# Last attention product of an eight-core transformer block: softmax sums and output normalization kept in PSUM

## The reference, cut to what matters

```
def sandwich(x):
    y = attention(layernorm(x))            # q, k, v = linear; softmax(q k^T / 8 + mask) v; linear Wp
    x = x + layernorm(y)
    f = layernorm(x) @ W[idx] + b[idx]     # idx: argmax of log_softmax(logits) + gumbel(u)
    return x + layernorm(f)
# mask: causal, and every fourth key column (3, 7, 11, ...) left out
```

## Time and profile before

| | |
|---|---|
| time before, median of 3 runs | 746.71 us (746.45 to 749.49) |
| the profiled execution's own time | 743.47 us |
| its span, core 6 (slowest) | 741.9 us |
| spans of the 8 cores | 740.7, 733.8, 737.9, 734.6, 741.3, 735.9, 741.9, 739.7 us |
| busy share of the span | PE 88%, ACT 72%, DVE 56%, POOL 19% |
| chain that ended last, by engine | PE 50%, ACT 15%, issue 15%, DMA 11%, DVE 6% |

### The profile page before, as it was taken

One profiled execution on the slowest core, in us unless ns is written; L12 is line 12 of the kernel. 1 busy time (PEld: TensorE's weight loads), 2 busy tenths in 40 slices (PEclk: granted clock), 3 DMA queues, 4 the chain that ended last, 5 costly groups with the idle time before them and its releaser, 6 DMA issues.

```text
span 741.3 us, 24579 instructions; the slowest of 8 cores (733.8 to 741.9 us)
## 1 busy us (share of the span) xinstructions
PE 649.0 (88%) x9452; PEld 283.8 (38%) x9460; DVE 418.1 (56%) x744; ACT 530.2 (72%) x718; POOL 144.0 (19%) x238
## 2 busy tenths in 40 slices
PE   1788989889898999999999998889999999999846
PEld 1444435344344444333433433333333333333312
DVE  3327766765655463653333333277766776986484
ACT  3233356344698787888878888888898989888246
POOL 1010013122122112212111124110120110760104
PEclk9979999899999999999999999999999999999989
DMA  8989467955357062123400035602233223142224
GB/s 161 185 184 159 147 173 154 208 83 109 99 115 165 18 132 44 32 46 55 93 17 17 18 59 84 190 16 74 83 77 88 75 88 105 34 138 87 102 57 142
DMA packets 78240, 72.47 MB, mean 98 GB/s; under 512 B 58544, under 2 KB 58800, under 8 KB 78128
## 3 DMA queue, kind: packets, MB, share of 16 engines
q1 hardware_dynamic: 72060, 59.50, 31.9%
q0 software_dynamic: 5696, 11.14, 9.6%
q10 hardware_dynamic: 372, 0.27, 0.2%
HBM read 60.68 MB, written 8.52 MB: 93 GB/s over the span
## 4 chain that ended last, share of the span: by engine, by line
PE 50%; ACT 15%; issue 15%; DMA 11%; DVE 6%; SPq 1%; ACTq 1%; POOL 1%; DVEq 0%; POOLq 0%
PE pj L673 23%; ACT Pr L1223 12%; PE sps L744 10%; PE yz L781 7%; PE yz L799 4%; DMA wkb<-wk 3%; DMA wvb<-wv 2%; PE yz L671 2%; DMA fmQ<-tok 1%; PE pj L671 1%; PE sps L847 1%; DVE Vsb L901 1%; DMA zr<-zev 1%; DMA xq<-xkv 1%; DMA xq<-xq 1%
## 5 line engine op out<-in xcount | busy, mean ns | idle before, releaser
L1223 ACT ACTIVATE Pr<-sps,negc 128x1024 bf16<-128x1024 f32 (+1 forms) x416 | 428.8, 1078 | 92.7 <-PE sps L746 90.1
L1354 POOL TENSOR_TENSOR Pr<-Pr,mk_sb 128x172 bf16<-128x172 bf16 x192 | 98.9, 536 | 464.8 <-ACT Pr L1223 464.7
L744 PE MATMUL sps<-QY,Ksb 64*128 64x512 bf16 (+2 forms) x480 | 138.7, 346 | 25.2 <-ACT Pr L1223 23.2
L746 PE MATMUL sps<-QY,Ksb 64*128 64x512 bf16 (+2 forms) x480 | 140.4, 350 | 0.0
L781 PE MATMUL yz<-Pr,Vsb 128*32 128x512 bf16 (+5 forms) x1920 | 125.0, 345 | 5.8 <-POOL Pr L1354 3.2
L744 PEld LDWEIGHTS sps<-QY,Ksb 64*128 64x128 bf16 x480 | 35.8, 93 | 133.5 <-issue 131.2
L799 PE MATMUL yz<-Pr,cbf 128*32 128x512 bf16 (+2 forms) x960 | 82.0, 345 | 0.0
L781 PEld LDWEIGHTS yz<-Pr,Vsb 128*32 128x32 bf16 x1920 | 49.4, 97 | 49.3 <-issue 12.5
L901 DVE TENSOR_TENSOR Vsb<-pj,bvb 128x512 bf16<-128x512 f32 x41 | 28.1, 688 | 52.4 <-PE pj L673 46.7
L673 PE MATMUL pj<-wpb,QY 128*32 128x512 bf16 x768 | 50.7, 381 | 0.1
L673 PE MATMUL pj<-fmQ,wqb 128*32 128x512 bf16 x768 | 48.0, 388 | 2.2 <-DMA fmQ<-tok 2.2
(11 more groups left out here) (195 smaller groups left out, 807.8 us busy)
## 6 DMA issues: line engine op xcount, KB each, us to landing
xin<-xkv SPq DMA_DIRECT2D x21, 512.0 KB, 4.7
xr<-xq SPq DMA_DIRECT2D x16, 512.0 KB, 3.4
zb<-zscr SPq DMA_DIRECT2D x62, 128.0 KB, 3.3
xin<-xq SPq DMA_DIRECT2D x12, 512.0 KB, 4.4
out<-xr SPq DMA_DIRECT2D x12, 512.0 KB, 2.8
wkb<-wk POOLq DMA_DIRECT2D x4, 512.0 KB, 17.8
wvb<-wv POOLq DMA_DIRECT2D x2, 1024.0 KB, 15.8
wqb<-wq POOLq DMA_DIRECT2D x2, 1024.0 KB, 14.2
```

What stands on the lines that cost most here:

```text
L744: PE.matmul(sps[s % 2][:, 0, off:off + w], Ksb[0:64, g, hp, kc:kc + 128], QY[0:64, t, hp, n0:n0 + w], start=True, stop=True, tile_position ...
L746: mm = PE.matmul(sps[s % 2][:, 1, off:off + w], Ksb[64:128, g, hp, kc:kc + 128], QY[64:128, t, hp, n0:n0 + w], start=True, stop=True, tile ...
L1223: A.activation(out=Pr[:, s % 4, :, 0:wide], in_=sps[s % 2][:, :, 0:wide], func=AF.Exp, bias=negc[:, k:k + 1], scale=0.125).then_inc(s_exp, 1)
L1354: op = G.tensor_tensor(out=view, in0=view, in1=mk[:, j:j + 1, :].broadcast_to([128, 2, BAND]), op=ALU.mult)
```

## The change

In product 31 the sums are laid out as the values are: for each step and each of the four groups of 32 partitions a matmul with the block of ones (`last_rowsum`), so that `zps` holds at each place the sum that belongs to the value at that place of `yps`. VectorE then takes the reciprocal from PSUM and multiplies, for 128 query columns at a time (`last_norm`); the copies and transfers of product 31 are gone. `tail_o` ends both halves of a subtile right after it has begun them. The masks of the last pass, 207, go from GpSimd to VectorE (`last_mask`). The end of every queue is no longer given by planned times but listed entry by entry (`behind`). The offsets of products 0 to 30 are written out rounded.

```diff
--- before.py
+++ after.py
@@ -256,11 +256,12 @@
             dve.append((x + 0.2, "fadd", u[1:]))
             if u[2] == 1:
                 f_free = x + 1.2 + 6.1
-                dve.append((x + 1.2, "fstat", u[1]))
-                act.append((x + 1.2 + 4.0, "froot", u[1]))
-                dve.append((x + 1.2 + 6.0, "final", u[1]))
-                sp.append((x + 1.2 + 9.0, "store", u[1]))
-                if u[1] + 4 < 16:
+                if u[1] < 11:
+                    dve.append((x + 1.2, "fstat", u[1]))
+                    act.append((x + 1.2 + 4.0, "froot", u[1]))
+                    dve.append((x + 1.2 + 6.0, "final", u[1]))
+                if u[1] < 10:
+                    sp.append((x + 1.2 + 9.0, "store", u[1]))
                     sp.append((x + 1.2 + 12.0, "resid", u[1] + 4))
     for s in range(4):
         sp.append((start[3] - 1.0 + 0.01 * s, "resid", s))
@@ -293,36 +294,34 @@
         for a in range(2):
             x = begin[m] + 0.4 + 1.1 * a
             act.append((x, "exp", 2 * m + a))
-            if masked(2 * m + a):
+            if masked(2 * m + a) and m < NP - 1:
                 pool.append((x + 1.1, "mask", 2 * m + a))
-    for k in range(32):
-        x = begin[LAST[k] + 2] if LAST[k] + 2 <= NP else begin[NP] + 1.0
+    for k in range(31):
+        x = begin[LAST[k] + 2]
         dve.append((x, "ycopy", k))
-        by, late = (sp, 1.35) if k < 31 else (act, 1.0)
-        by.append((x + 1.4, "zrow", k))
-        dve.append((x + 4.2 * late, "zinv", k))
-        by.append((x + 4.6 * late, "zout", k))
-        by.append((x + 7.6 * late, "zback", k))
+        sp.append((x + 1.4, "zrow", k))
+        dve.append((x + 5.7, "zinv", k))
+        sp.append((x + 6.2, "zout", k))
+        sp.append((x + 10.3, "zback", k))
         again = begin[LAST[k + 2] + 2] - 0.3 if k < 29 else begin[NP] + 20.0
-        dve.append((min(x + 13.5 * late, again), "ynorm", k))
-
-    at = begin[NP] + 16.0
-    z_at, x_at, f_at, last_at = [0.0, 1.4, 5.2, 9.0], [2.8, 6.6, 10.4, 12.8], [15.2, 16.6, 18.0, 22.0], [17.2, 18.6, 20.2, 24.0]
-    for j, s in enumerate(TAIL):
-        dve.append((at + z_at[j], "tailz", s))
-        act.append((at + z_at[j] + 1.4, "tailzroot", s))
-        dve.append((at + x_at[j], "tailx", s))
-        act.append((at + x_at[j] + 2.4, "tailln", s))
-        sp.append((at + x_at[j] + 4.5, "turn", s))
-        dve.append((at + f_at[j], "tailfs", s))
-        act.append((at + f_at[j] + 1.4, "tailfroot", s))
-        if s < 15:
-            act.append((at + last_at[j], "tailscale", s))
-            pool.append((at + last_at[j] + 0.6, "tailsum", s))
-        else:
-            dve.append((at + last_at[j], "taillast", s))
-            act.append((at + last_at[j] + 0.6, "tailout", s))
-        sp.append((at + last_at[j] + 1.2, "tailstore", s))
+        dve.append((min(x + 18.2, again), "ynorm", k))
+
+
+    late = max(begin[NP], max(item[0] for item in dve)) + 1.0
+
+    def behind(queue, *items):
+        queue.extend((late + 0.01 * n, kind, key) for n, (kind, key) in enumerate(items))
+
+    behind(dve, ("lastmask", 0), ("lastmask", 1), ("fstat", 11), ("lastnorm", 12), ("lastnorm", 13), ("lastnorm", 14),
+           ("tailz", 12), ("lastnorm", 15), ("tailx", 12), ("tailz", 13), ("final", 11), ("tailx", 13), ("tailz", 14),
+           ("tailz", 15), ("tailx", 14), ("tailx", 15), ("tailfs", 12), ("tailfs", 13), ("tailfs", 14), ("tailfs", 15),
+           ("taillast", 15))
+    behind(act, ("froot", 11), ("tailzroot", 12), ("tailln", 12), ("tailzroot", 13), ("tailln", 13), ("tailzroot", 14),
+           ("tailzroot", 15), ("tailln", 14), ("tailln", 15), ("tailfroot", 12), ("tailscale", 12), ("tailfroot", 13),
+           ("tailscale", 13), ("tailfroot", 14), ("tailscale", 14), ("tailfroot", 15), ("tailout", 15))
+    behind(pool, ("tailsum", 12), ("tailsum", 13), ("tailsum", 14))
+    behind(sp, ("store", 10), ("resid", 14), ("turn", 12), ("store", 11), ("resid", 15), ("turn", 13), ("turn", 14),
+           ("turn", 15), ("tailstore", 12), ("tailstore", 13), ("tailstore", 14), ("tailstore", 15))
     for i in range(3):
         pool.append((begin[FIRST[30]] + 1.0 + 9.0 * i, "biasrow", i))
     pool.append((-400.0, "weights", 0))
@@ -565,6 +564,8 @@
     s_zout = sem("s_zout")
     s_zback = [sem(f"s_zback{i}") for i in range(2)]
     s_ynorm = sem("s_ynorm")
+    s_lastmask = sem("s_lastmask")
+    s_lastinv = sem("s_lastinv")
     s_res = [sem(f"s_res{i}") for i in range(4)]
     s_zadd = sem("s_zadd")
     s_zbn = sem("s_zbn")
@@ -766,7 +767,9 @@
                 if k > 0:
                     PE.wait_ge(s_ycopy, k)
             for s in (2 * m, 2 * m + 1):
-                if masked(s):
+                if s >= 2 * NP - 2:
+                    PE.wait_ge(s_lastmask, s - 2 * NP + 3)
+                elif masked(s):
                     PE.wait_ge(s_mask, MASK_N[s])
                 else:
                     PE.wait_ge(s_exp, s + 1)
@@ -781,12 +784,27 @@
                             PE.matmul(yps[j:j + 32, n0:n0 + w], Vsb[:, c, 64 * h + 32 * half:64 * h + 32 * half + 32],
                                       Pr[:, s % 4, hd, off:off + w], start=first, stop=final, tile_position=(0, j))
 
+        def last_rowsum(m):
+
+            for s in (2 * m, 2 * m + 1):
+                for c, n0, w, off in STEPS[s][1]:
+                    first = s == 2 * FIRST[31]
+                    final = s == 2 * LAST[31] + 1 and off + w == 428
+                    for j in (0, 32, 64, 96):
+                        mm = PE.matmul(zps[j:j + 32, n0:n0 + w], cbf[:, 288:320], Pr[:, s % 4, j // 64, off:off + w],
+                                       start=first, stop=final, tile_position=(0, j))
+            return mm
+
         def rowsum(m):
 
             k, _ = STEPS[2 * m]
             first, final = m == FIRST[k], m == LAST[k]
             if first and k > 0:
                 PE.wait_ge(s_zcopy, k)
+            if k == 31:
+                mm = last_rowsum(m)
+                mm.then_inc(s_pv, 1)
+                return
             if first and k < 8:
                 for hd in range(2):
                     PE.matmul(zps[64 + 32 * hd:96 + 32 * hd, :], cbf[:, 320:352], Pr[:, 2 * m % 4, hd, :],
@@ -824,19 +842,12 @@
             if s == 14:
                 PE.wait_ge(s_exp, 2 * NP)
             if s == 15:
-                PE.wait_ge(s_ycopy, 32)
-                PE.wait_ge(s_zcopy, 32)
+                PE.wait_ge(s_ynorm, 35)
             tail_begin(s, 0)
-            if s < 15:
-                tail_begin(s, 1)
-            else:
-                PE.wait_ge(s_ynorm, 32)
-                for r in (12, 13, 14):
-                    tail_end(r, 0)
-                    tail_end(r, 1)
-                tail_end(15, 0)
-                tail_begin(15, 1)
-                tail_end(15, 1)
+            tail_begin(s, 1)
+            PE.wait_ge(s_ynorm, s + 20)
+            tail_end(s, 0)
+            tail_end(s, 1)
 
         def tail_f(s):
             PE.wait_ge(s_tturn[s - 12], 16)
@@ -990,6 +1001,25 @@
             t, hp = k // 8, k % 8
             V.wait_ge(s_zback[k % 2], 32 * (k // 2 + 1))
             V.tensor_tensor(out=QY[:, t, hp, :], in0=yev[:, k % 2, :], in1=zb[:, k % 2, :],
+                            op=ALU.mult).then_inc(s_ynorm, 1)
+
+        def last_mask(a):
+            s = 2 * NP - 2 + a
+            V.wait_ge(s_mk, 16)
+            V.wait_ge(s_exp, s + 1)
+            for c, _, _, off in STEPS[s][1]:
+                view = Pr[:, s % 4, :, off:off + BAND]
+                op = V.tensor_tensor(out=view, in0=view, in1=mk[:, c - 18:c - 17, :].broadcast_to([128, 2, BAND]),
+                                     op=ALU.mult)
+            op.then_inc(s_lastmask, 1)
+
+        def last_norm(s):
+
+            n0, n1 = 128 * (s - 12), 128 * (s - 11)
+            V.wait_ge(s_pv, NP)
+            V.reciprocal(out=zev[:, 1, n0:n1], in_=zps[:, n0:n1]).then_inc(s_lastinv, 1)
+            V.wait_ge(s_lastinv, s - 11)
+            V.tensor_tensor(out=QY[:, 3, 7, n0:n1], in0=yps[:, n0:n1], in1=zev[:, 1, n0:n1],
                             op=ALU.mult).then_inc(s_ynorm, 1)
 
         def zadd(key):
@@ -1143,6 +1173,10 @@
                 fstat(key)
             elif kind == "final":
                 final(key)
+            elif kind == "lastmask":
+                last_mask(key)
+            elif kind == "lastnorm":
+                last_norm(key)
             elif kind == "tailz":
                 tail_z(key)
             elif kind == "tailx":
@@ -1307,22 +1341,6 @@
                 x1root(key)
             elif kind == "froot":
                 froot(key)
-            elif kind == "zrow":
-                A.wait_ge(s_zcopy, key + 1)
-                for a in range(2):
-                    A.dma_start(out=zr[:, key % 2, a, :], in_=zev[64 * a:64 * a + 64:32, key % 2, :]
-                                ).then_inc(s_zrow[key % 2], 16)
-            elif kind == "zout":
-                A.wait_ge(s_zinv, key + 1)
```

(9 more changed lines are left out.)

## The result

The changed kernel takes 741.78 us (median of 5 runs, 740.27 to 742.84) against 746.71 us (745.7 to 749.49), a ratio of 0.9927 with a 95% interval of 0.9902 to 0.9952: 0.7% faster, 742.5 was forecast. The profiled execution took 742.84 us.

A forecast was written before the change was run, and what follows sets the result against it. TensorE mostly sets the pace before the tail; in it product 31's DRAM trip, then VectorE's queue, bound the kernel. Terms +0.9 before the tail, −6.1 in it, +1.0 clock: −4.2 us, median 742.5, range 738.0 to 747.2.

The forecast's parts named there:

- What bounds what: In the tail, after the change, VectorE's queue from the norms to tailx 15 is what is late.
- the trip's 12.7 us: Product 31's copies and DRAM transfers: removing them isn't 12.7 us gained, since 56 of 64 opening matmuls ran meanwhile.
- Sums: Product 31's passes before the tail: doubled sum matmuls cost +1.4 us, bounds +0.7 to +2.3.
- P: Start of the tail's first matmul, 691.29 us before the change; forecast to move by +0.9 us.
- Masks: Last pass: masks on VectorE take about 0.3 us each and bring P −0.5 us, bounds −0.8 and 0.
- Norms: Tail on VectorE: reciprocal 1.1 us, wait 0.1, multiply 0.3, so 1.5 us for each of four subtiles.
- Clock: TensorE's clock in the tail: three new pauses may slow F 14, up to 2.5 us; allowed +1.0.
- Sum: Whole kernel: +0.9 before P, −6.1 after it, +1.0 for the clock, −4.2 us, median 742.5.
- Queue order: Rounded offsets swap zback 6 and feature 28 on SP; costs nothing, 1.3 us at most without cover.
- A: Rival in the tail: reciprocal takes only 0.36 us, later steps gain 2.5, −6.7 us, 740.0; chance 0.17.
- B: Rival in the tail: TensorE stays at 1.2 GHz through F, slower than before, 751.7; chance 0.06.
- C: Rival in the tail: reciprocal takes 2 us and sums the full +2.3, leaving about 0, 746.5; chance 0.15.

The follow-up runs named there:

- experiment 5: Changed kernel with each of the four reciprocals issued twice; P to the end 46.9 to 47.6 us on four cores, 48.5 to 49.0 on four.
- experiment 8: Changed kernel with tailz 14 earlier and final 11 moved from VectorE to ScalarE and GpSimd; 736.25 us, ratio 0.9914 to the kernel before.
- experiment 2: Changed kernel with output halves in the old order (12, 13, 14 all begun, then ended, then 15); ratio 1.0012 to the kernel before.
- experiment 3: Changed kernel with only half the sum matmuls in product 31's nine full passes; that stretch 24.01 to 24.02 us, P to the end 43.57 to 44.03.
- experiment 1: Changed kernel with the last pass's masks back on GpSimd; q-k products to the end 47.77 us, against 47.76 with masks on VectorE.
- experiment 6: Changed kernel with eleven useless matmuls in each TensorE pause before F 13 and F 14; P to the end 44.12 us.
- experiment 4: Changed kernel with copies of the same size instead of the four reciprocals; P to the end 43.13 us, −0.94.
- experiment 10: The changed kernel run again, unaltered, beside the best version; 740.16 us, ratio 0.9931 to the kernel before.
- experiment 7: Changed kernel, reordered only: tailz 14 ahead of final 11 and tailx 13, its root ahead of tailln 13; ratio 0.9933 to the kernel before.
- experiment 9: Final 11 off VectorE with tailz 14 earlier, plus eight useless matmuls in TensorE's pause before F 13; 736.19 us, ratio 0.9887 to the kernel before.

## Why the prediction was right, step by step

- *What bounds what.* VectorE's queue from the norms to tailx 15 is late, as forecast: experiments 5 (+3.2 at F 13 for longer norms) and 8 (−1.9 for 2.2 us less) move the end from that queue; experiment 2 shows the other half of the statement, that the trip's 12.7 us were no gain while TensorE's opening matmuls stood ahead of the first end.
- *Sums.* Forecast +1.4 in all, between +0.7 and +2.3; measured +1.09 up to the last q-k products, which experiment 3 takes away exactly, and 0.19 from there to P (4.31 in experiment 1 against 4.12), 1.28 in all. The first part holds the nine full passes, priced at 9 × 0.22: 0.9 of these 1.98 us were swallowed. Of that the rows show 0.4 as idle time that went (TensorE is idle 1.66 of 24.02 us before and 1.30 of 25.10 after); where the rest went, they don't show, as ends of matmuls are modelled. The second part holds the sums of passes 206 and 207, priced at 0.18 and 0.15; those of 206 end before TensorE waits for the last masks, and cost nothing.
- *Masks.* Forecast −0.5 in P, with 0.3 given back behind it: fstat 11 ends at P + 0.9, "the sums are there at 0.6, as now". The operation was sized right (0.24 each against 0.3) and P came sooner by 0.62, but the step that failed is this 0.6. Before the change it was the start of the copy of the values; the reciprocal could start 0.16 us after P (experiment 1), and behind fstat it started at 0.77. So 0.61 us are given back of 0.62, and the masks' term is 0 for the end instead of −0.2.
- *Norms.* Forecast 1.1 + 0.1 + 0.3, measured 0.94 + 0.1 + 0.29, and the next instruction starts slightly before the end: 1.26 from one norm to the next instead of 1.5. That is nearly all of the difference in the chain: tailz 12 at 4.53 (5.45), F 12 at 16.3 (17.4), F 13 at 22.8 (24.05), F 14 at 29.1 (30.4), the end at 43.6 on core 4 (44.5 without the clock). The median end is 44.07, as on five cores F 15's turn comes 0.1 to 0.5 us after F 14 is done, a wait that the prediction did not have. The reciprocal grows with its length: 16 values (from SBUF, 64 partitions) 0.244 us, 128 values (from PSUM, 128 partitions) 0.94, 6.2 ns more for each. Of the two rules of the Trainium skill that the prediction set against each other ("VectorE: DVE Perf Modes"), the formula of its errata section, an estimate of 0.26 us, fits the copy (0.27) and not the reciprocal; the divide repeated 8 times, an estimate of 1.07 us and more, is the nearer one, though the measured 0.94 lies below it.
- *Clock.* Forecast +1.0, measured about 0 for the end. F 13 was the slow one and covered: F 14 starts at the same time after P with it slow or quick, and experiment 6, with both quick, ends no sooner. That a slow F 14 costs 1.5 us and more was right and shows in experiments 4 and 5. Not forecast: before, P to the end is 1.3 to 2.1 us longer on the three cores with a slow clock after P; after, all are within 0.75 us.
- *Sum.* P moved by +1.28 − 0.62 = +0.66 (+0.9 forecast), the tail by −5.2 (−6.1 + 1.0 forecast). That the sum comes within 1 us is in part luck. The end was forecast 45.5 us after P and came at 44.07, 1.4 too late, from the norms' price and the clock; but it was taken from the 50.6 of core 6, one of the three with the slow clock after P, where the median core had 49.27, 1.3 less. The two errors cancel. On core 6 itself the tail became 6.8 us shorter, not 5.1.
- *Queue order.* No run separates the rounded offsets of products 0 to 30. Product 30's last values start at 660.6 us before (median of the cores), 662.4 after and 660.5 in experiment 10, single cores anywhere from 656 to 669: no cost stands out of that spread, and none is excluded below it.
- *Rivals.* A (cheap reciprocal) would have been worth 0.94 us against the measured kernel, or 1.4 against the forecast 44.5, not the 2.5 that it was given (experiment 4): TensorE's output and the root of tailz 12 take over at once. B (a slow clock through F) did not come. C (a reciprocal of 2 us) is nearly what experiment 5 imitates: P to the end is 46.9 to 49.0 there against 49.27 before, and P comes 0.66 us later, which would have left little.

## What to carry to other kernels

Taking a round trip off a path frees only what was not being used meanwhile: what ran under the wait (here 56 matmuls) must be cut into pieces whose first result starts the next stage, or the gain is gone (experiment 2). An operation moved from an idle engine to the one that is late is priced by that engine's queue, not by the wait that it shortens. When a queue is the bound, look for work in it that idle engines can do, even in more steps: 2.2 us moved from VectorE to ScalarE and GpSimd (4.6 us there) gave 1.9. And a forecast that starts from the slowest core should first ask whether that core's stretch is the others' too: here 1.3 us of its tail were not.

## What the runs showed of the hardware

- A reciprocal of 128 float32 values from PSUM takes 0.93 to 0.95 us, a copy of the same tile 0.27, the multiply 0.29.
- A 2 × 86 mask in bfloat16 takes 0.24 us on VectorE, 0.46 to 0.55 on GpSimd.
- After a pause of 2.5 us TensorE's next F half took 2.7 to 3.6 us on six cores and 1.94 on two of the same execution (the changed kernel, F 13); after one of 4.0 us 3.4 to 3.8 on all eight (experiment 7); with eight matmuls without use in the pause 1.94 on all eight (experiment 9). Why before the change three cores had a clock of 0.5 after P and in experiment 1, with the same masks on GpSimd, none had, stays open: each is one execution. The rows show one difference, that TensorE's idle time ahead of the last pass's first values is 1.25 us before and 1.06 in experiment 1, behind the doubled sums.
